# Four graph layers on one core: the third layer's end and the fourth's preparation unrolled in three batches

## The reference

```python
# third layer, after the sums over each node's incoming edges
out = (sum_of_weighted_V / (attn_sum + 1e-16)) @ Wo + bo      # attn_sum per node and head
h = out + concat(x, type_emb[node_type]) @ Wskip
h = elu(layer_norm(h) * gamma + beta)
x = layer_norm(x + h)
# fourth layer, before its edges
C = 0.5 * (cos(edge_weight * pi / 10) + 1)                     # one cutoff per edge
h = x @ lin1_w.T                                               # the rows that edges gather
```

## Time and profile before

| what | us |
|---|---|
| median of 3 runs (lowest, highest) | 9314.26 (9308.85, 9314.34) |
| the profiled execution | 9289.43 |
| its span | 9287.6 |
| busy in the span: POOL, PE, DVE, ACT | 6125.4, 5336.4, 4895.6, 1745.2 |

### The profile page before, as it was taken

How to read it: one execution, slowest core, us unless ns; L and a number is a source line. 1 busy time by engine, 2 the same in 40 slices (tenths; PEclk the granted TensorE clock), 3 DMA queues, 4 the chain that set the end, 5 groups by cost and what they waited for, 6 DMA issues and landing times. The chain is left out here.

```text
span 9287.6 us, 88604 instructions
## 1 busy us (share of the span) xinstructions
PE 5336.4 (57%) x27633; PEld 4325.2 (47%) x27633; DVE 4895.6 (53%) x10581; ACT 1745.2 (19%) x2599; POOL 6125.4 (66%) x6479
## 2 busy tenths in 40 slices
PE   4555555553344444444466666666435888887884
PEld 3444444442233333333355555555423555555553
DVE  5666666656422222222477777777654554555555
ACT  0000000002100000000300000000013555555553
POOL 5777777770377777777277777777403777777772
PEclk6666666665555555555677777777656878888886
DMA  5433434430233333333255555555301222222221
GB/s 172 115 114 111 115 110 115 113 105 2 57 77 77 75 77 76 75 77 75 84 166 164 164 165 164 164 164 164 91 1 52 73 74 74 72 74 72 74 73 36
DMA packets 391598, 906.48 MB, mean 98 GB/s; under 512 B 134405, under 2 KB 202936, under 8 KB 368288
## 3 DMA queue, kind: packets, MB, share of 16 engines
q0 software_dynamic: 232704, 538.22, 22.7%
q1 hardware_dynamic: 153538, 351.59, 12.6%
q10 hardware_dynamic: 4896, 11.01, 0.3%
HBM read 867.89 MB, written 32.45 MB: 97 GB/s over the span
## 5 line engine op out<-in xcount | busy, mean ns | idle before, releaser
L2117 POOL DMA_INDIRECT TMP<-schnet_table,src_idx x1616 | 1535.3, 950 | 964.1 <-issue 491.9
L1631 POOL DMA_INDIRECT PM<-hgt_kv_table,src_idx x1616 | 1528.0, 946 | 640.5 <-issue 467.0
L634 POOL DMA_INDIRECT PM<-gat_table,src_idx x1616 | 1531.8, 948 | 546.1 <-issue 492.2
L1177 POOL DMA_INDIRECT PM<-gcn_table,src_idx x1004 | 950.6, 947 | 306.0 <-issue 304.4
L1177 POOL DMA_INDIRECT TMP<-gcn_table,src_idx x612 | 577.3, 943 | 550.5 <-POOLq L1038 364.3
L1205 PE MATMUL ps<-TMP,PM 128*128 128x128 f32 x2008 | 515.5, 438 | 702.5 <-DMA PM<-gcn_table,src_idx 702.3
L1252 DVE TENSOR_TENSOR AC<-AC,ps 128x128 f32 x101 | 29.1, 288 | 1522.2 <-PE ps L1205 1522.2
L679 PE MATMUL ps<-PM 128*128 128x139 f32 x3232 | 781.2, 433 | 66.8 <-DVE PM L773 66.5
L1205 PEld LDWEIGHTS ps<-TMP,PM 128*128 128x128 f32 x2008 | 443.7, 325 | 763.8 <-DMA PM<-gcn_table,src_idx 626.9
L679 PEld LDWEIGHTS ps<-PM 128*128 128x128 f32 x3232 | 739.4, 327 | 73.1 <-DVE PM L773 72.8
L2144 PE MATMUL ps<-PM 128*128 128x128 f32 x3232 | 542.4, 321 | 362.6 <-issue 206.3
(11 more groups left out here) (383 smaller groups left out, 9008.2 us busy)
## 6 DMA issues: line engine op xcount, KB each, us to landing
PM<-local_dst_row SPq DMA_DIRECT2D x101, 1024.0 KB
PM<-local_dst_row SPq DMA_DIRECT2D x202, 512.0 KB, 3.9
PM<-in_attrT SPq DMA_DIRECT2D x101, 400.0 KB
xT<-in_rel_row SPq DMA_DIRECT2D x101, 384.0 KB, 4.8
PM<-gat_table,src_idx POOLq DMA_INDIRECT x1616
PM<-hgt_kv_table,src_idx POOLq DMA_INDIRECT x1616, 3.0
TMP<-schnet_table,src_idx POOLq DMA_INDIRECT x1616, 2.5
PM<-gcn_table,src_idx POOLq DMA_INDIRECT x1004, 2.5
```

What stands on the lines that cost most here:

```text
L634: pool.indirect_dma_start(out=g[:, par, t, 0:TAB0], out_offset=None, in_=tab0_d, in_offset=bass.IndirectOffsetOnAxis(ap=src_idx[:, i * ROU ...
L1177: pool.indirect_dma_start(out=g[n % DEEP][:, k, :], out_offset=None, in_=tab1_d, in_offset=bass.IndirectOffsetOnAxis(ap=src_idx[:, n * KT ...
L1631: pool.indirect_dma_start(out=g[:, par, t, 0:2 * P], out_offset=None, in_=kv_d, in_offset=bass.IndirectOffsetOnAxis(ap=src_idx[:, i * ROUN ...
L2117: pool.indirect_dma_start(out=g[:, b, k, :], out_offset=None, in_=tab3_d, in_offset=bass.IndirectOffsetOnAxis(ap=src_idx[:, (i * SLOTS + b ...
```

## The change

It replaces the loop over five chunks and the two blocks behind it by one block without loops. The denominators of all tiles are transposed (33 rows to 33 columns a tile), inverted as 8 numbers per node, spread to 128 columns by a ScalarE copy, and transposed back onto the numerators. The skip rows are made in the second layer's end, as 128 more columns of the K, V, Q product, and kept in xT, tile by tile with nodes on partitions; bo is added to the type rows. Layer norms go by bn_stats and by tile; the fourth layer's table rows follow in the same block, batch by batch. The cutoff is now 1 minus the square of a sine and made on GpSimd. gamma, beta and the fourth layer's weights are loaded at the start of the third layer's edge loop. The fourth layer's cutoff lies in TMP in place of PM.

The diff, cut, with eight columns of indentation taken off; of the new block only the added lines stand (the lines it replaces are described above):

```diff
-t8, t8b = A.take(3 * P, parts=NTYPE), A.take(3 * P, parts=NTYPE)
+t8, t8b = A.take(4 * P, parts=NTYPE), A.take(4 * P, parts=NTYPE)
...
-emb_T, T8s = cols[:, 0:NTYPE], rows[0:NTYPE, 0:P]
-T8b = WA[0:TY, 0:3 * P // 2].bitcast(BF16)
+emb_T, out_bias = cols[:, 0:NTYPE], rows[0:NTYPE, 0:P]
+T8b = WA[0:TY, 0:2 * P].bitcast(BF16)
...
+        sp.dma_start(out_bias, a["L2_gnn_bo"].partition_broadcast(NTYPE)).then_inc(hp_ld, 16)
...
-        pe.wait_ge(hp_ld, 160)
+        pe.wait_ge(hp_ld, 176)
...
-            s.mark(dve.tensor_copy(T8s, PS[3][0:NTYPE, 0, 3 * P:4 * P]))
-            s.link(dve.tensor_copy(t8, PS[3][0:NTYPE, 0, 0:3 * P]))
+            s.mark(dve.tensor_copy(t8[:, 0:3 * P], PS[3][0:NTYPE, 0, 0:3 * P]))
+            s.link(dve.tensor_tensor(t8[:, 3 * P:4 * P], PS[3][0:NTYPE, 0, 3 * P:4 * P], out_bias, ALU.add))
...
+skip = xT[:, :].rearrange("p (t f) -> p t f", f=P)
...
-        engine.wait_ge(ev_act, acts)
+        engine.wait_ge(ev_act, 2 * acts)
     if dves:
-        engine.wait_ge(ev_dve, dves)
+        engine.wait_ge(ev_dve, 2 * dves)
...
-                ps = PS[2 + t_ % 4 // 2][:, t_ % 2, 0:3 * P]
-                nc.tensor.matmul(ps, xT[:, t_ * P:(t_ + 1) * P], WB[:, 0:3 * P], start=True, stop=False, skip_group_check=True)
+                ps = PS[2 + t_ % 4 // 2][:, t_ % 2, :]
+                nc.tensor.matmul(ps, xT[:, t_ * P:(t_ + 1) * P], WB[:, 0:4 * P], start=True, stop=False, skip_group_check=True)
                 nc.tensor.matmul(ps, oh8b[:, t_ * P:(t_ + 1) * P], T8b, start=False, stop=True, skip_group_check=True).then_inc(kvq_mm, 1)
...
+                    nc.scalar.copy(skip[:, t_, :], PS[2 + t_ % 4 // 2][:, t_ % 2, 3 * P:4 * P]).then_inc(ev_act, 1)
...
+                    dve.tensor_copy(skip[:, t_, :], PS[2 + t_ % 4 // 2][:, t_ % 2, 3 * P:4 * P]).then_inc(ev_dve, 1)
...
+        for dst_, src_ in ((gamma, row_bc("L2_gnn_gamma")), (beta, row_bc("L2_gnn_beta")), (lin1, a["L3_gnn_lin1_w_T"]), (w1, a["L3_gnn_mlp_w1_T"]),
+                           (w2, a["L3_gnn_mlp_w2_T"]), (lin2, a["L3_gnn_lin2_w_T"]), (linw, a["L3_gnn_lin_w_T"]), (b1, col_in("L3_gnn_mlp_b1")),
+                           (l2b, col_in("L3_gnn_lin2_b")), (brow, a["L3_gnn_mlp_b2"].rearrange("(o f) -> o f", o=1))):
+            sp.dma_start(dst_, src_).then_inc(late, 16)
         either(sp, program)
+        sp.wait_ge(late, 160)
...
+        sp.dma_start(cw, a["w_et"]).then_inc(w_ld, 16)
+        for n in range(GROUPS4):
+            sp.wait_ge(row_copied, n + 1)
+            sp.dma_start(tab3_d[columns_of(n), :].rearrange("(t p) f -> p t f", p=P), y[:, nodes_of(n), :]).then_inc(stored, 16)
+        sp.wait_ge(stored, 16 * GROUPS4)
+    @block.gpsimd
+    def _(pool):
+        s = Steps(pool, cd)
+        pool.wait_ge(w_ld, 16)
+        s.link(pool.tensor_scalar(wk, cw, 0.05, None, ALU.mult))
+        s.link(pool.tensor_copy(wq, wk))
+        s.link(pool.tensor_scalar(wq, wq, -20.0, None, ALU.mult))
+        s.link(pool.tensor_tensor(wq, wq, cw, ALU.add))
+        pool.wait_ge(cs, 1)
+        s.link(pool.tensor_tensor(wq, wq, wq, ALU.mult))
+        s.link(pool.tensor_scalar(cw, wq, -1.0, 1.0, ALU.mult, ALU.add))
+    @block.tensor
+    def _(pe):
+        for k in range(4):
+            at, ps = sums_t(k)
+            for t_ in range(at.start, at.stop):
+                m = nc.tensor.transpose(ps[:, t_ - at.start, :], acc2[0:ZW, 1, t_ * P:(t_ + 1) * P], ident[0:ZW, 0:ZW])
+            m.then_inc(z_t, 1)
+        nc.tensor.matmul(PS[3][0:1, 0, 0:P], ones[:, 0:1], w2, start=True, stop=True).then_inc(bt, 1)
+        def turn_inverse(n):
+            pe.wait_ge(wide, n + 1)
+            if n >= 2:
+                pe.wait_ge(num_ready, n - 1)
+            for k, t_ in enumerate(tiles_of(n)):
+                m = nc.tensor.transpose(group_ps(4 + n % 2, n)[:, k, :], y[:, t_, :], ident[:, :])
+            m.then_inc(turned_r, 1)
+        def products(n):
+            pe.wait_ge(num_ready, n + 1)
+            if n >= 2:
+                pe.wait_ge(out_read, n - 1)
+            if n == 0:
+                pe.wait_ge(fs, 1)
+            for k, t_ in enumerate(tiles_of(n)):
+                m = nc.tensor.matmul(group_ps(6 + n % 2, n)[:, k, :], acc2[:, 0, t_ * P:(t_ + 1) * P], WB[:, 4 * P:5 * P], start=True, stop=True)
+            m.then_inc(out_mm, 1)
+        def turn_x(n):
+            pe.wait_ge(normed, tiles_of(n)[-1] + 1)
+            if n >= 2:
+                pe.wait_ge(x_copied, n - 1)
+            for k, t_ in enumerate(tiles_of(n)):
+                m = nc.tensor.transpose(group_ps(n % 2, n)[:, k, :], xn[:, t_, :], ident[:, :])
+            m.then_inc(x_t, 1)
+        def row_products(n):
+            pe.wait_ge(x_copied, n + 1)
+            if n >= 2:
+                pe.wait_ge(row_copied, n - 1)
+            for k, t_ in enumerate(tiles_of(n)):
+                m = nc.tensor.matmul(group_ps(2 + n % 2, n)[:, k, :], xT[:, t_ * P:(t_ + 1) * P], lin1, start=True, stop=True)
+            m.then_inc(row_mm, 1)
+        for lo, hi in BATCHES:
+            turn_inverse(lo)
+            for n in range(lo, hi):
+                if n + 1 < hi:
+                    turn_inverse(n + 1)
+                products(n)
+        for lo, hi in BATCHES:
+            turn_x(lo)
+            for n in range(lo, hi):
+                if n + 1 < hi:
+                    turn_x(n + 1)
+                row_products(n)
     @block.scalar
     def _(act):
+        def spread_inverse(j):
+            act.wait_ge(inverse, j + 1)
+            for n in range(*BATCHES[j]):
+                at = nodes_of(n)
+                nc.scalar.copy(y[:, at, :].rearrange("p t (h c) -> p t h c", c=C2), over(rz[:, at, :], P, at.stop - at.start, H2, C2)).then_inc(wide, 1)
+        def rstds(j, k):
+            at = span_of(BATCHES[j])
+            act.wait_ge(var_ready[k], j + 1)
+            nc.scalar.activation(w["rstd"][:, at], w["var"][:, at], ACT.Ln).then_inc(rstd_ln[k], 1)
+            act.wait_ge(rstd_ln[k], j + 1)
+            nc.scalar.activation(w["rstd"][:, at], w["rstd"][:, at], ACT.Exp, scale=-0.5).then_inc(rstd_ready[k], 1)
+        def exps(j):
+            for n in range(*BATCHES[j]):
+                act.wait_ge(y_ready, n + 1)
+                nc.scalar.activation(t[:, nodes_of(n), :], y[:, nodes_of(n), :], ACT.Relu, scale=-1.0).then_inc(elu_ln, 1)
+            for n in range(*BATCHES[j]):
+                act.wait_ge(elu_ln, n + 1)
+                nc.scalar.activation(t[:, nodes_of(n), :], t[:, nodes_of(n), :], ACT.Exp, scale=-1.0).then_inc(elu_ready, 1)
+        def norm(j):
+            act.wait_ge(scaled, j + 1)
+            for t_ in tiles_in(BATCHES[j]):
+                nc.scalar.activation(xn[:, t_, :], t[:, t_, :], ACT.Identity, scale=w["rstd"][:, t_:t_ + 1], bias=w["shift"][:, t_:t_ + 1]).then_inc(normed, 1)
+        def keep_x(n):
+            act.wait_ge(x_t, n + 1)
+            nc.scalar.copy(skip[:, nodes_of(n), :], group_ps(n % 2, n)).then_inc(x_copied, 1)
+        def keep_rows(n):
+            act.wait_ge(row_mm, n + 1)
+            nc.scalar.copy(y[:, nodes_of(n), :], group_ps(2 + n % 2, n)).then_inc(row_copied, 1)
+        def finish(lo, hi):
+            keep_x(lo)
+            for n in range(lo, hi):
+                if n + 1 < hi:
+                    keep_x(n + 1)
+                keep_rows(n)
+        act.wait_ge(aged, 5)
+        nc.scalar.activation(age, age, ACT.Exp).then_inc(age_exp, 1)
+        spread_inverse(0)
+        spread_inverse(1)
+        rstds(0, 0)
+        spread_inverse(2)
+        exps(0)
+        rstds(1, 0)
+        rstds(0, 1)
+        rstds(2, 0)
+        norm(0)
+        exps(1)
+        finish(*BATCHES[0])
+        act.wait_ge(cd, 4)
+        nc.scalar.activation(wq, wq, ACT.Sin, scale=float(np.pi) / 20).then_inc(cs, 1)
+        rstds(1, 1)
+        exps(2)
+        norm(1)
+        finish(*BATCHES[1])
+        rstds(2, 1)
+        norm(2)
+        finish(*BATCHES[2])
     @block.vector
     def _(dve):
+        s = Steps(dve, fs)
+        def filter_bias():
+            s.mark(dve.memset(capc, SP_CAP))
+            s.mark(dve.tensor_scalar(cap1, b1, -1.0, SP_CAP, ALU.mult, ALU.add))
+            s.mark(dve.tensor_scalar(cap2, l2b, -1.0, SP_CAP, ALU.mult, ALU.add))
+            s.mark(dve.memset(bsplit, 0.0))
+            s.mark(dve.memset(ones_b, 1.0))
+            s.settle()
+            for j in range(3):
+                part_ = bsplit[32 * j:32 * j + 1, :].rearrange("p (k f) -> p k f", f=P)
+                s.link(dve.tensor_copy(part_, brow.unsqueeze(1).to_broadcast([1, KT, P])))
+                s.link(dve.tensor_copy(bres, part_[:, 0, :]))
+                s.link(dve.tensor_tensor(brow, brow, bres, ALU.subtract))
+        def inverses(j):
+            at = span_of(BATCHES[j])
+            s.link(dve.reciprocal(rz[:, at, :], rz[:, at, :]))
+            dve.sem_inc(inverse, 1)
+        def attended(j):
+            def numerators(n):
+                dve.wait_ge(turned_r, n + 1)
```

(87 more changed lines are left out.)

217 lines of the change are left out of this document (35 added, 182 removed).

## The result

| | before | after |
|---|---|---|
| median on one chip | 9312.82 us (9308.85 to 9314.34, 4 runs) | 9027.16 us (9026.44 to 9029.15, 4 runs) |
| ratio of the medians, 95% interval | | 0.9694 [0.9677, 0.9711] |
| the profiled execution, its span | 9289.43, 9287.6 | 9027.80, 9025.8 |
| busy POOL, PE, DVE, ACT | 6125.4, 5336.4, 4895.6, 1745.2 | 6159.4, 5296.0, 4797.4, 1743.0 |

The change makes the kernel 285.7 us faster. For the profiled execution alone the sum had given 9029, and it took 9027.80; why that agreement is luck is said further down.

The account below looks back on a forecast made before the run. GpSimd's gathers pace the edge loops; between the third and fourth, a serial chain of engines takes 453.2 us. Cutting it to 175 saves 278, less 15 and 3 elsewhere: 260, so a median of 9054 us, range 9028 to 9102.

Parts of the forecast that it names:

- the named stretch: Third layer's last edge instruction to fourth layer's first gather, a serial chain between engines; 453.2 us was to become 175.
- the price elsewhere: Costs outside the shortened gap: 15 us in the second layer's end, 3 us for late loads and bias load.
- The rival on the other side: Fourth layer's loop: TensorE's clock settles lower and sets the pace, slower than before from a clock of 0.60; chance 0.02.
- (b): Start of the new block: 50 transposes of the sums with 33 columns, and the bias product, 9 us.
- (e): Attended phase, three batches in 13 groups of VectorE passes and TensorE transposes and products; 45 us, 38.5 to 51.5.
- (g): End of attended(2) to end of norm(1), VectorE and ScalarE chains side by side; 43 us, from 41.9 to 45.2.
- (h): finish(1): four groups of TensorE transposes and products with ScalarE's copies between; 10 us, 8.5 fast, 13.7 slow.
- (j): finish(2), the last batch's finish before the store; 12.5 us, between 10.5 and 16.
- hand-overs: Some twenty passes of work between engines in the new block, only partly in the rows; 6 us, 0 to 12.
- the second rival: New block: GpSimd's six cutoff instructions hold VectorE up, 22 us if it stands still during each, median 9076; chance 0.12.
- the first-placed case: New block with TensorE's clock mixed between 0.50 and 1.00: 175 us, saving 260, median 9054; chance 0.55.
- the fast clock from the start: New block with TensorE's clock up throughout: 158 us plus 3, price 13, saving 279, median 9035; chance 0.07.

## Why the prediction was right, and where it was wrong

**The mechanism was right.** The time came from the named stretch, 453.2 to 158.6, and nothing in the loops became dearer than executions differ. Of the 25.7 us by which the saving of 285.7 exceeds the 260 of the sum, 16.6 lie in the stretch (294.6 for 278), 3.3 in the price elsewhere (14.8 for 18), and 5.8 in neither. The rival on the other side (a lower clock in the fourth loop) fell: 0.80, where 0.60 was the point from which it would decide. The batches overlap as assumed.

**The steps of the sum**, us as put in the prediction (its fast and slow ends) and as the first profile after gives them:

| step | taken | measured |
|---|---|---|
| (a) entry | 3.3 | 3.0 |
| (b) transposes and bias product | 9 (7.5 to 14) | 5.8 |
| (c) reference, age, inversions | 5.6 | 8.5, 2.9 of it the hold |
| (d) filter bias | 4.1 | 7.7, 3.8 of it the hold |
| (e) attended | 45 (38.5 to 51.5) | 36.1 |
| (f) first_norm(0), residual(0) | 20.5 | 20.2 |
| (g) to the end of norm(1) | 43 | 45.1, 4.0 of it the hold |
| (h) finish(1) | 10 (8.5 to 13.7) | 8.8 |
| (i) rstds, scales, norm(2) | 11.1 | 11.2 |
| (j) finish(2) | 12.5 (10.5 to 16) | 7.9 |
| (k) store to first gather | 5.0 | 4.3 |
| hand-overs | 6 | 0 |
| sum | 175 | 158.6 |

**The step that failed** is the size of a term and not the mechanism: TensorE's price in (e), (h) and (j), and with it the choice between two clocks. I took 2.5 us for four products at half clock and 1.25 at full, from one record's 0.63, and 3.6 for a group of the attended phase. The record's 0.63 holds a start-up that overlapped records don't pay again: in the burst above such records start 0.43 apart. Four products take 2.08 or 1.06, and from one cold group to the next it is 2.52 us (the weight loads of the two start at 6707.03 and 6709.55), close to VectorE's own 2.2. So (e) came out at 36.1, under my fast end, although all of its three batches began cold (L1964 2.08, 2.07 and 2.08 for the first four products), and (j) at 7.9. VectorE is busy for 28.0 us of (e); my fast end had 31.3 for that (13 groups at 2.2 and three variances at 0.9). The dispute over the clock, on which I put 0.55 against 0.22 against 0.07, was worth far less than the 27 us between my ends. These three terms were 14.7 us too dear together; how they share it moves with the execution, since finish(1) and finish(2) traded 1 us between two profiles of the same kernel.

**Two more terms were too dear.** The hand-overs were 6 us without a row: VectorE's rows follow each other, and where it waits the wait was already in a term. (b) is 5.29 us for 50 transposes, 0.106 each and almost all at the clock of 0.50, where I took 0.16. My two ends, 0.60 / 4 and 1.12 / 4, are what one transpose with 128 columns takes at either clock; one with 33 columns costs less than that even at the lower clock, so the low end of 7.5 was no bound.

**GpSimd's hold was the second rival, and it happened beside the first-placed case instead of in its place.** At 10.7 us it is half of the 22 put on it. The six instructions take 18.2 us and not 22, and only certain forms of VectorE's are held: the reciprocals ran beside GpSimd freely. That the first 9 us would lie under TensorE's transposes was wrong: GpSimd waited for the edge weights until 6689.85, when the transposes (6684.27 + 5.29 = 6689.56) were over. It hid the other error in part: without it the stretch is 149.5, below the 158 that I had called the fast clock from the start. Giving this rival 0.12 as a case of its own was wrong; it should have been a term of the sum in every case.

**The price elsewhere.** 15 us for the second layer's end: measured 14.8, and 14.4 by taking the columns away. The 3 us for late loads and bias load: none found, since the first of the third loop's work had slack; the second loop, with the bias load ahead of it, took 2018.7 to 2018.9 us in six of the profiles of changed kernels, against 2019.1 and 2019.2 before.

**The range.** 294.60 less 14.76 is 279.84 us from the two gaps. The other 5.8 of the median's 285.66 lie in no step, and they are what put the result below the range: the low end's own terms (a stretch of 158, a price of 13) allow a saving of 282. They give 9032, and no term says where the lower 9028 came from. The 5.8 came back on other chips as 2.7 (284.1 against 281.4) and 6.4 (287.2 against 280.8, with the gaps of before from the other chips). The one profiled execution of before on those chips has a fourth loop of 2031.9 against 2027.3 to 2032.6 in the kernels after, so this is not settled; two profiles of the kernel before are too few to tell a faster loop from chance. My low end allowed nothing for it. It was my last step, the sum made against one profiled execution and its distance of 24.8 us carried over to the median, that took no account of how executions differ. The same step made 9029 against 9027.80 look exact: the gaps saved 19.8 us more than the 260 of the sum, and loops that happened to be 17.0 longer in this execution took most of it back.
